# Moving the next image's statistics into the second convolution, and another order of what feeds both convolutions

## The chip, the core and the metric

One core of one Trainium2 chip runs the whole program: TensorE (PE, with its weight loads PEld), VectorE (DVE), ScalarE (ACT), GpSimd (POOL) and SyncE (SP), with 16 DMA engines. POOL issues transfers on the software queue q0, SP on the hardware queue q1. The metric is the device time of one launch in microseconds (us), as the median of several.

## The reference

The input x is 8 images of 96 channels x 96 x 96, all float32. Two blocks are applied in a row, each with a residual and a group norm (`_gn`, 32 groups of 3 channels) ahead of it:

```python
# block 0: four depthwise convolutions in four directions, mixed by a softmax, then a full 3x3 convolution
feats = stack([feat_h, feat_v, feat_d45, feat_d135])      # 7 taps each, per channel
context = mean(feats * feats, (3, 4))
attn = softmax(leaky_relu(context @ w_att1.T, 0.2) @ w_att2.T over the 4 directions)
x = x + conv3x3(sum(attn * feats), w_proj)
# block 1: linear attention whose output passes a 1x1, a depthwise 3x3 and further 1x1 matrices
x = x + _L1(_gn(x))
```

## The kernel before

**Two blocks, pipelined over images.** Call the images b = 0 to 7. A step of the loop does block 0 of image b and block 1 of image b-1 side by side. Each block ends in a 3x3 convolution on PE, written in `conv` (L1048). It runs over NG = 12 row groups of 8 rows; a row group j is two halves of 4 rows, and a half is 9 matmuls on `e_hi`, 9 on `e_lo` and 3 on `shifted`. The **second convolution** (weights `a1, a2, a3`, source line L1064 with `a`) closes block 1 of image b-1; the **first convolution** (weights `wp1, wp2, wp3`, L1064 with `wp`) closes block 0 of image b and comes right after it on PE.

**One step in time.** (1) PE runs the attention work of image b-1 while DVE adds taps of image b (L806: 4 directions, 6 taps each, in 12 units of 12 taps; a unit is two directions of one of NCH = 6 chunks of 16 rows). (2) PE runs the second convolution, DVE units 9 to 11, and between its taps DVE splits the exponentials into `e_hi` and `e_lo` (`e_split`, 24 tiles, the last 14 here). (3) `hidden` and `logits` (L1215, L1222) are small matmuls that PE does at row group 11 of the second convolution, between its halves; DVE waits for them in `attention` and turns them into the four mixing factors. (4) `products` (L928, L938) mix the four directions chunk by chunk: the feature maps come back from DRAM (`feats_d`, 20 loads of 576 KB by SP), the sum goes to the buffer `acc`, ACT rounds it to `e_hi` (`fg_high`, L669), DVE computes `e_lo` (`fg_low`, L944). (5) PE runs the first convolution on them. After each row group DVE adds the residual (`x1_sum`, L896) and takes statistics (L900). `SUMS_AFTER` says how many of these stand behind each chunk's products, the rest follow in `start`. (6) `start` of the next image: six loads of x into `feat` (L378), sums and sums of squares by ACT (`x_sums`, L531, two passes a load), group norm on DVE with one small matmul on PE (L1046) and one power on POOL (L416), then `norm_chunk` (L553) and `first_tap` (L573) on ACT, and the first 20 taps on DVE, with the rest of the `x1_sum` between them. (7) The group norm of the sum x1 (L765 on), and the next attention begins.

**Order.** Each engine runs its instructions in the order of its program; there is no scheduler. What links them is semaphores. For a row group j of either convolution PE waits (`ready`) for five transfers by POOL (`fill`, L426): two bulk copies of 32 partitions (L431, L432) and three ring transfers into `shifted` (L435), whose two slots come free when row group j-2 is done. From row group 2 on the second convolution also waits for `final_copy` (L651) of group j-2 on ACT, the first for `x1_sum` of group j-2 on DVE. POOL, behind each fill, also issues the stores of results and, in the first convolution, the loads of the residual (`res`). The buffer at `arena2` is shared in time by `s1`, `a32` and `acc`.

**What holds the change.** On ACT `final_copy` calls stand between `unit_work` of units 9, 10 and 11, which takes the squares of a unit (L585) and so waits for DVE's last taps of it.

## Time and profile before

| | us |
|---|---|
| median of 3 runs | 4011.15 (4006.11 to 4013.85) |
| the profiled execution | 4010.97 |
| its span | 4009.3 |
| PE busy | 3374.3 (84%) |
| DVE busy | 2954.0 (74%) |
| ACT busy | 1791.1 (45%) |
| POOL busy | 694.5 (17%) |

Times in the rows below are from the span's start. What the profiled execution adds to its span is 1.7 us, and it is within 0.2 us of the median. One full step (image 4, from 2009 us to 2480 us) is read closely; the others repeat it.

### The profile page before, as it was taken

To read this page: it belongs to the slowest core of one execution; us is meant where nothing else is said; L and a number is where in the kernel's file an instruction comes from. 1 tells how busy PE (TensorE), PEld (TensorE's weight loads), DVE (VectorE), ACT (ScalarE), POOL (GpSimd) and SP (SyncE) were. 2 spreads that over 40 slices of the span, in tenths; PEclk is the share of its full clock that TensorE was granted. 3 is DMA by queue.
4 is the path that set the end of the run, shared out by engine and by line. 5 is a ranking of instruction groups with operands and counts; after the bars stand their busy time and mean duration, and the time that the engine had idled before them with its cause. 6 is when DMAs were issued, how large, how long until landed. Compare 5 with 4: busy or idle time off the path is not lost.

```text
span 4009.3 us, 56727 instructions
## 1 busy us (share of the span) xinstructions
PE 3374.3 (84%) x20626; PEld 2713.3 (68%) x20626; DVE 2954.0 (74%) x2721; ACT 1791.1 (45%) x2921; POOL 694.5 (17%) x1336
## 2 busy tenths in 40 slices
PE   4648998699976999679986899869997799968998
PEld 2336687568765687666875677756876668757787
DVE  6976987579865998569984698758986599844211
ACT  5423682238623384135831467223861348410550
POOL 1013003220132102230022200322013200223003
PEclk9768999799998999889997999979998899989999
DMA  4367224943259324692338622494235923376004
GB/s 105 94 145 179 64 74 84 212 120 79 70 103 234 80 74 90 133 214 62 74 80 181 165 65 74 92 225 113 68 83 109 221 78 78 78 146 151 1 11 86
DMA packets 210824, 440.70 MB, mean 110 GB/s; under 512 B 125696, under 2 KB 125936, under 8 KB 210512
## 3 DMA queue, kind: packets, MB, share of 16 engines
q1 hardware_dynamic: 141392, 255.36, 26.3%
q0 software_dynamic: 69120, 181.32, 21.3%
q8 instruction: 179, 2.93, 0.3%
q14 instruction: 133, 1.09, 0.1%
HBM read 189.27 MB, written 150.99 MB: 85 GB/s over the span
## 4 chain that ended last, share of the span: by engine, by line
PE 31%; DVE 31%; issue 24%; DMA 10%; ACT 2%; POOL 1%; DVEq 0%; SPq 0%; ACTq 0%; POOLq 0%
DVE feat L806 22%; DMA feat<-feats_d 8%; PE banks L1083 6%; PE banks L1064 4%; PE banks L1069 4%; PE banks L1093 3%; PE banks L1151 3%; PE banks L1113 2%; PE banks L1099 2%; PE banks L1100 2%; DVE acc L938 2%; DVE feat L938 2%; DVE x L896 1%; PE banks L1073 1%; DMA shifted<-e_hi 1%
## 5 line engine op out<-in xcount | busy, mean ns | idle before, releaser
L806 DVE SCALAR_TENSOR_TENSOR feat<-xin,w,feat 96x1536 f32<-96x1536 f32 x540 | 947.0, 1807 | 1.8
L1064 PE MATMUL banks<-e_hi,wp 128*96 128x384 f32 x1728 | 397.5, 382 | 356.2 <-DMA shifted<-e_hi 240.5
L1064 PEld LDWEIGHTS banks<-e_hi,wp 128*96 128x96 f32 x1728 | 314.2, 186 | 408.0 <-issue 243.5
L585 ACT ACTIVATE squares<-feat 96x1536 bf16<-96x1536 f32 x192 | 285.1, 1485 | 589.2 <-DVE feat L806 587.0
L806 DVE SCALAR_TENSOR_TENSOR feat<-xin,wh,feat 96x1536 f32<-96x1536 f32 x288 | 520.3, 1807 | 30.1 <-ACT feat L573 28.4
L806 DVE SCALAR_TENSOR_TENSOR feat<-xin,wv,feat 96x1536 f32<-96x1536 f32 x288 | 520.3, 1807 | 0.0
L1064 PE MATMUL banks<-e_hi,a 128*96 128x384 f32 x1728 | 360.9, 356 | 106.7 <-ACT res L651 106.0
L1064 PEld LDWEIGHTS banks<-e_hi,a 128*96 128x96 f32 x1728 | 289.8, 170 | 149.5 <-ACT res L651 96.7
L1069 PE MATMUL banks<-e_lo,wp 128*96 128x384 f32 (+1 forms) x1728 | 369.7, 363 | 0.0
L1069 PE MATMUL banks<-e_lo,a 128*96 128x384 f32 (+1 forms) x1728 | 350.4, 349 | 0.0
L1069 PEld LDWEIGHTS banks<-e_lo,wp 128*96 128x96 f32 x1728 | 310.2, 180 | 32.6
L1093 PEld LDWEIGHTS banks<-mats,z 96*96 96x96 f32 x3072 | 287.3, 165 | 57.5 <-issue 46.7
L1069 PEld LDWEIGHTS banks<-e_lo,a 128*96 128x96 f32 x1728 | 292.5, 170 | 29.1
L1137 PE MATMUL banks<-wkv,x 97*96 97x96 f32 x3072 | 295.9, 249 | 0.9
L669 ACT ACTIVATE e_hi<-acc 96x1536 fp32r<-96x1536 f32 x48 | 71.4, 1488 | 497.6 <-DVE acc L938 497.6
L1093 PE MATMUL banks<-mats,z 96*96 96x96 f32 x3072 | 289.8, 248 | 2.5 <-ACT z L614 2.5
L435 POOL DMA_DIRECT2D shifted<-e_hi x576 | 285.7, 517 | 9.6 <-issue 9.4
L1137 PEld LDWEIGHTS banks<-wkv,x 97*96 97x96 f32 x3072 | 278.6, 165 | 10.4 <-issue 6.0
L421 POOL MEMSET e_hi<- 96x97 f32 x9 | 1.6, 176 | 1498.0 <-PE banks L1153 1498.0
L431 POOL DMA_DIRECT2D e_hi<-e_hi x192 | 100.1, 521 | 824.2 <-PE banks L1073 410.6
L651 ACT ACTIVATE res<-banks 96x768 f32<-96x768 f32 x96 | 74.8, 801 | 358.8 <-PE banks L1073 358.8
L815 DVE TENSOR_REDUCE mx<-banks 96x1 f32<-96x512 f32 x288 | 185.1, 681 | 42.1 <-PE banks L1083 41.9
(161 smaller groups left out, 5456.3 us busy)
## 6 DMA issues: line engine op xcount, KB each, us to landing
feats_d<-feat SPq DMA_DIRECT2D x160, 576.0 KB, 4.1
feat<-feats_d SPq DMA_DIRECT2D x160, 576.0 KB, 8.4
shifted<-e_hi POOLq DMA_DIRECT2D x576, 97.2 KB, 2.7
feat<-in_x SPq DMA_DIRECT2D x48, 576.0 KB, 9.5
res<-in_x POOLq DMA_DIRECT2D x96, 288.0 KB, 4.7
out<-x POOLq DMA_DIRECT2D x96, 288.0 KB, 2.9
out<-res POOLq DMA_DIRECT2D x96, 288.0 KB, 4.4
xin<-in_x SPq DMA_DIRECT2D x32, 792.0 KB, 8.7
```

The lines of the kernel that those rows point to most:

```text
L431: pool.dma_start(e_hi[C:C + SPARE, lo:hi], e_hi[0:SPARE, lo:hi]).then_inc(done, 16)
L435: pool.dma_start(shifted[g * SPARE:(g + 1) * SPARE, j % 2, :], e_hi[2 * SPARE:C, at:at + SHIFTED])\
L585: act.activation(squares[0 if first_image(b) or u <= LEAD else 1][:], feat[:, d], ACT.Square, accum_out=sq[:, d, ch:ch + 1]).then_inc(squa ...
L806: dve.scalar_tensor_tensor(out=dst, in0=src, scalar=taps_w[d](k), in1=dst, op0=ALU.mult, op1=ALU.add).then_inc(tap_done, 1)
L815: dve.tensor_reduce(mx[:, n % 2, n // 2:n // 2 + 1], stage_ps[0:C, n % SLOTS, :], AX.X, ALU.max)\
L938: ins = dve.scalar_tensor_tensor(out=flat if k == DIRS - 1 else part, in0=feat[:, d], scalar=l0v[:, 8 + d:9 + d], in1=part, op0=ALU.mult, ...
L1064: pe.matmul(dst, w1[:, t, :], rows(e_hi, a0, n, dx, 128), start=(t == CENTRE_FIRST[0]), stop=False)
L1069: pe.matmul(dst, w2[:, t, :], rows(e_lo, a0, n, dx, 128), start=False, stop=False)
L1083: pe.matmul(ps[0:C, :], w, x1[0:C, t * BANK:(t + 1) * BANK], start=True, stop=True)\
L1093: last = pe.matmul(ps[0:H, c * W:(c + 1) * W], z[:, 4 * g + c, :], w_dft, start=(c == 0), stop=(c == 3), skip_group_check=True)
L1137: last = pe.matmul(ps[0:W, r * C:(r + 1) * C], x1[:, h * W:(h + 1) * W], wkv[:, part * C:(part + 1) * C], start=(r == 0), stop=(r == TR - ...
L1151: pe.matmul(gram_ps[0:C, 2 * C:4 * C], t_sp[:, v, 0:C], t_sp[:, v, :], start=(v == 1), stop=(v == NV - 2))
```

## The change

- **ACT's order in the second convolution.** The final copies stand 3, 4, 3 ahead of the work of units 9, 10, 11 where 2, 2, 2 stood (`COPIES_AFTER`).
- **The next image's x.** Its six loads go no longer to `feat` at the end of the step but, one at a time, to `xc`, which lies where `acc` lies; ACT sums them after the final copies 1, 3, 4, 5, 7 and 8 (`CHUNKS_AT`). The passes' other output goes to PSUM, no longer to `squares`. SP issues the first after `a32` is free, each further one after the sums of the one before; the stores of unit 9 stand between the second and the third. The first write of `acc` waits for the last sums. Only image 0 keeps the old way.
- **The fills.** The three ring transfers of a row group come first, and the two bulk copies behind them are those of the next row group; each kind has its own semaphores.
- **DVE.** `SUMS_AFTER` is 0, 0, 1, 2, 1, 1 for 0, 0, 0, 1, 1, 1; the group norm of x stands after six `x1_sum`, where it stood after five, and PE's matmul for it goes to row group 7. The tiles of `e_split` stand behind taps 1, 2, 4, 5, 7, 8, 10, 11 of a unit, where they stood behind 2, 4, 6, 8, 10, 12.

```diff
-SUMS_AFTER = (0, 0, 0, 1, 1, 1)
-GN_AT = sum(SUMS_AFTER) + 2
+SUMS_AFTER = (0, 0, 1, 2, 1, 1)
+GN_AT = sum(SUMS_AFTER) + 1
+CHUNKS_AT = (1, 3, 4, 5, 7, 8)
+COPIES_AFTER = (3, 7, 10)
...
+        xc = nc.alloc_sbuf_tensor_at("xc", [C, CR * W], F32, offset=s0)
...
+            def load_xc(b, n, second):
+                x = image(a["x"], b + 1)
+                if n >= 1:
+                    sp.wait_ge(x_stat, 2 * ((b + 1) * NCH + n))
+                elif second:
+                    sp.wait_ge(l1_small, b * L1_SMALL)
+                else:
+                    sp.wait_ge(wp_ready, LO_PARTS)
+                sp.dma_start(xc[:], x[:, n * CR * W:(n + 1) * CR * W]).then_inc(xc_loaded, 16)
...
                 for u in range(UNITS - 2):
+                    if more and u == UNITS - 3:
+                        load_xc(b, 0, second)
+                        load_xc(b, 1, second)
...
+                for n in range(2, NCH if more else 0):
+                    load_xc(b, n, second)
...
             def fill_e(i, j):
...
-                fill(e_filled, j)
+                e_rows(i, j)
+                shift(e_shifted, j)
+                for n in range(0 if j == 0 else j + 1, min(NG, j + 2)):
+                    e_rows(i, n)
+                    copy(e_copied, n)
...
+            def x_sums(b, n, x, junk):
+
+                for k, func in enumerate((ACT.Identity, ACT.Square)):
+                    wait(act, x_stat, 2 * (b * NCH + n) + k)
+                    act.activation(junk, x, func, accum_out=xsums[:, k, n:n + 1]).then_inc(x_stat, 1)
+
+            def next_x_sums(b, n):
+                act.wait_ge(xc_loaded, (b * NCH + n + 1) * 16)
+                x_sums(b + 1, n, xc[:].rearrange("p (b n) -> p b n", n=BANK), stage_ps[0:C, 2:SLOTS])
...
             def start(b):
-                if not first_image(b):
-                    x_sums(b)
                 norm_chunk(b, 0)
...
                 for u in range(LEAD + 1, UNITS):
-                    copies(j, j + 2)
-                    j += 2
+                    for n in range(j, COPIES_AFTER[u - LEAD - 1]):
+                        copies(n, n + 1)
+                        if more and n + 1 in CHUNKS_AT:
+                            next_x_sums(b, CHUNKS_AT.index(n + 1))
+                    j = COPIES_AFTER[u - LEAD - 1]
                     if first:
                         unit_work(b, u)
...
                         if k == DIRS - 1:
+                            if ch == 0 and more:
+                                dve.wait_ge(x_stat, 2 * (b + 2) * NCH)
+                                apart(dve)
```

ACT in the second convolution of a full step, before, from the second final copy on (L651; L585 squares, L573 first taps of unit 11):

```order
L651 ACTIVATE res<-banks 96x768
L583 REGISTER_ALU
L585 ACTIVATE squares_64,sq<-feat 96x1536
L583 REGISTER_ALU
L267 REGISTER_ALU
L585 ACTIVATE squares_64,sq<-feat 96x1536
L573 ACTIVATE feat<-xin,w 96x1536
L565 REGISTER_ALU
L573 ACTIVATE feat<-xin,w 96x1536
L648 REGISTER_ALU
L651 ACTIVATE res<-banks 96x768
```

The same place of the changed kernel (L686 is the final copy, L561 the sums, L620 the squares):

```order
L686 ACTIVATE res<-banks 96x768
L683 REGISTER_ALU
L686 ACTIVATE res<-banks 96x768
L564 REGISTER_ALU
L270 ISA
L561 ACTIVATE banks,xsums<-xc 96x1536
L270 REGISTER_ALU
L561 ACTIVATE banks,xsums<-xc 96x1536
L618 REGISTER_ALU
L620 ACTIVATE squares_65,sq<-feat 96x1536
```

The third final copy and the sums of one load of x now stand ahead of unit 9's squares.

DVE between the products of chunks 3 and 4 of a full step, before (L938 products, L928 the next chunk's first, L944 `fg_low`, L896 and L900 `x1_sum`):

```order
L938 SCALAR_TENSOR_TENSOR acc<-feat,l0v 96x1536
L926 ISA
L928 TENSOR_SCALAR feat<-feat,l0v 96x1536
L944 TENSOR_TENSOR e_lo<-acc,e_hi 96x16x96
L893 ISA
L894 ISA
L896 TENSOR_TENSOR x<-banks,res 96x768
L900 BN_STATS x1stats<-x 96x6 x2
```

There, in the changed kernel (L977, L964, L983, L932 and L936 are the same operations):

```order
L977 SCALAR_TENSOR_TENSOR acc<-feat,l0v 96x1536
L964 TENSOR_SCALAR feat<-feat,l0v 96x1536
L982 REGISTER_ALU
L983 TENSOR_TENSOR e_lo<-acc,e_hi 96x16x96
L929 REGISTER_ALU
L932 TENSOR_TENSOR x<-banks,res 96x768
L936 BN_STATS x1stats<-x 96x6 x2
L929 REGISTER_ALU
L932 TENSOR_TENSOR x<-banks,res 96x768
L936 BN_STATS x1stats<-x 96x6 x2
```

Before, this is the first `x1_sum`; now it is the second and the third, and the first stands one chunk earlier.

POOL in the middle of the second convolution, before (one row group and its store):

```order
L431 DMA e_hi<-e_hi 32x776
L432 DMA e_lo<-e_hi 32x776
L435 DMA shifted<-e_hi 32x778 x3
L480 ISA
L480 DMA out<-res 96x768
```

The same in the changed kernel:

```order
L444 DMA shifted<-e_hi 32x778 x3
L456 REGISTER_ALU
L452 DMA e_hi<-e_hi 32x776
L453 DMA e_lo<-e_hi 32x776
L512 ISA
L512 DMA out<-res 96x768
```

The ring transfers have moved ahead of the bulk copies, which are the next row group's.

## Rows read from the trace of the kernel before

**Rows 1.** The page: the chain that ended last, share of the span by engine.

```profile
PE 31%; DVE 31%; issue 24%; DMA 10%; ACT 2%; POOL 1%; DVEq 0%; SPq 0%; ACTq 0%; POOLq 0%
```

**Rows 2.** Waits, whole span: waiter, its releaser, us in total, times, longest.

```profile
DVE hid L909 <- PE banks L1215: 179.5, 8, 26.2
...
PE banks L1064 <- ACT res L651: 106.0, 21, 8.3
```

**Rows 3.** PE, second convolution, image 4: start, us, instructions [idle before <-releaser].

```profile
2028.63 1.70 PE L1064 MATMUL banks<-e_hi,a 128*96 128x384 f32 x9
...
2062.60 2.44 PE L1064 MATMUL banks<-e_hi,a 128*96 128x384 f32 x9 [4.13 <-ACT res L651]
...
2107.00 3.19 PE L1064 MATMUL banks<-e_hi,a 128*96 128x384 f32 x9 [6.77 <-ACT res L651]
...
2131.47 0.52 PE L1215 MATMUL banks<-l0v,att 96*48 96x1 f32 x8
```

**Rows 4.** PE, the last second convolution (image 7), its first and last matmuls.

```profile
3905.98 1.70 PE L1064 MATMUL banks<-e_hi,a 128*96 128x384 f32 x9 [0.26 <-DVE a L742]
...
3994.56 0.69 PE L1073 MATMUL banks<-shifted,a 96*96 96x384 f32 x3
```

**Rows 5.** ACT in the second convolution, image 4.

```profile
2054.27 1.49 ACT L585 ACTIVATE squares<-feat 96x1536 bf16<-96x1536 f32 x1 [9.89 <-DVE feat L806]
...
2060.28 1.57 ACT L573 ACTIVATE feat<-xin,w 96x1536 f32<-96x1536 f32 x1 [0.46 <-DMA feats_d<-feat]
2061.76 1.48 ACT L651 ACTIVATE res<-banks 96x768 f32<-96x768 f32 x2
```

**Rows 6.** PE, first convolution: four rows of image 4, one of image 7.

```profile
2156.61 2.95 PE L1064 MATMUL banks<-e_hi,wp 128*96 128x384 f32 x9 [16.31 <-DMA shifted<-e_hi]
...
2179.83 0.71 PE L1073 MATMUL banks<-shifted,wp 96*96 96x384 f32 x3
2190.05 3.19 PE L1064 MATMUL banks<-e_hi,wp 128*96 128x384 f32 x9 [9.52 <-DVE x L896]
...
2217.18 3.19 PE L1064 MATMUL banks<-e_hi,wp 128*96 128x384 f32 x9 [5.16 <-DMA shifted<-e_hi]
...
3613.59 3.17 PE L1064 MATMUL banks<-e_hi,wp 128*96 128x384 f32 x9 [11.64 <-DVE x L896]
```

**Rows 7.** DVE from the products on, image 4.

```profile
2138.10 1.01 DVE L928 TENSOR_SCALAR feat<-feat,l0v 96x1536 f32<-96x1536 f32 x1
...
2189.05 0.95 DVE L896 TENSOR_TENSOR x<-banks,res 96x768 f32<-96x768 f32 x1
...
2211.18 1.76 DVE L944 TENSOR_TENSOR e_lo<-acc,e_hi 96x1536 fp32r<-96x1536 f32 x1 [1.56 <-ACT e_hi L669]
...
2235.47 0.16 DVE L758 TENSOR_REDUCE mv<-xsums 96x2 f32<-96x12 f32 x1 [7.04 <-ACT squares L531]
...
2239.11 0.16 DVE L782 SCALAR_TENSOR_TENSOR xpar<-gstat,xpar 96x1 f32<-96x1 f32 x1
...
2292.35 0.80 DVE L765 BATCH_NORM_AGGREGATE mv<-x1stats 96x2 f32<-96x144 f32 x1 [0.16 <-DVE x1stats L900]
```

**Rows 8.** Stretch, us, PE, PEld, DVE, ACT, POOL busy, PEclk, DMA share, GB/s.

```profile
2029.00:2140.00 111.00, 95.82 (x520) 85.69 (x518) 78.54 (x79) 21.22 (x27) 34.24 (x61) 0.94 0.45 86
```

**Rows 9.** DMA from 2029 to 2140 us: issues, KB each, median us to landing.

```profile
shifted<-e_hi POOLq DMA_DIRECT2D x30, 97.2 KB, 2.4
feats_d<-feat SPq DMA_DIRECT2D x2, 576.0 KB, 4.0
```

**Rows 10.** DMA from 2141 to 2211 us (products): total, queue's share, ring transfers.

```profile
DMA packets 3907, 16.72 MB, mean 239 GB/s; under 512 B 793, under 2 KB 793, under 8 KB 3904
...
q1 hardware_dynamic: 2330, 12.33, 73.0%
...
shifted<-e_hi POOLq DMA_DIRECT2D x15, 97.2 KB, 7.3
```

**Rows 11.** DMA from 2211 to 2240 us: one load of the next image's rows.

```profile
xin<-in_x SPq DMA_DIRECT2D x1, 792.0 KB, 19.8
```

91 lines of the change are left out of this document (47 added, 44 removed).

## The prediction

> **What bounds the kernel now.** I read the page's chain first: it is split evenly between PE and DVE [rows 1], so no engine's total is the limit, and each stretch of a step has to be read for the wait that ends last. The list of waits names two that hang together [rows 2]: in the second convolution PE waits 21 times (three times in each of images 1 to 7) for ACT's final copy, 106.0 us in all, and DVE waits 179.5 us for `hidden`, the small matmul that stands behind eleven row groups of that convolution. PE's rows give the size [rows 3]: the convolution starts at 2028.63 and reaches `hidden` at 2131.47, 102.8 us for eleven row groups. The same work without anything beside it takes 3995.25 - 3905.98 = 89.3 us for twelve, 7.45 us each [rows 4]. So 102.8 - 82.0 = 20.8 us per step are lost: about 15.2 us idle and the rest matmuls after each idle time at the lower clock (2.44 and 3.19 us for nine, against 1.70). ACT's rows say why [rows 5]: with the third row group finished, ACT stands at unit 9's squares, which DVE's taps release at 2054.27, then at a first tap that waits for a store until 2060.28, and copies only at 2061.76. The other two waits have the same cause at units 10 and 11.
>
> The first convolution is held by other things. Its start waits 16.31 us for its fills, its third row group 9.52 us for the first `x1_sum`, its fifth 5.16 us for a ring transfer [rows 6]. DVE's side [rows 7]: that `x1_sum` stands at 2189.05, one chunk late; the last `fg_low` at 2211.18; then DVE waits 7.04 us for ACT's sums of x, and from the factors of the group norm (2239.3) to the group norm of x1 (2292.35) it is DVE's own taps and sums that fill 53.1 us. The DMA engines are full in the products [rows 10]: 16.72 MB at 239 GB/s.
>
> **Change, second convolution (images 1 to 7).** Start PE at 2028.6, a row group every 7.45 us: groups 0 to 11 end at 2036.1, 2043.5, 2051.0, 2058.4, 2065.9, 2073.3, 2080.8, 2088.2, 2095.7, 2103.1, 2110.6, 2118. Group j+2 needs copy j. Now ACT: copies 0 to 2 and two loads' sums (two passes of 1.5 us each, like the squares [rows 5]) are done by 2054.9. Unit 9 ends on DVE 1.5 us later than before, since 8 splits of 0.74 us stand in it for 6, so its squares, the store and the first taps end near 2063.4; copy 3 is done at 2064.3, needed at 2065.9. That is the tightest place, 1.6 us. Copy 4 and the third load's sums fit before 2073.3. A load of 576 KB lands in about 4.0 us, as the stores do [rows 9], and is issued only after the sums before it, so a load and its sums take some 7.2 us, just inside a row group. Units 10 and 11 end near 2083 and 2104; copy 7 comes at 2089 (needed 2095.7), copy 9 at 2104 (2110.6). All three waits go. Unit 11's squares end at 2107.4, so `hidden` isn't late either: 2110.7. What is late next is DVE's taps with their squares, 3 us behind.
>
> What it may cost: the DMA engines. Their share is 0.45 of 111 us [rows 8], 50 us. Six loads add 3.5 MB; at 0.73 x 70 us for 12.33 MB [rows 10] that is 4.1 us of the engines per MB, 14.7 us. 65 us in 91 us, and near 0.85 in the row groups where a load is always under way. A ring transfer lands 2.4 us after its issue here [rows 9] and 7.3 us in the full stretch [rows 10]; issued 2.4 us after the group before last has ended, it is in time up to 5.0 us. The new order gives it 1 us that the two bulk copies took. Best case nothing, worst case 2.3 us in three groups: 0 to 7 us a step. I take 1.5 us, since the mean share stays under 1 and nearer to rows 9. Passes that write PSUM stand in no row; from the 1.49 us of the squares up to twice that there is room, since ACT has 21 us of work in 111 [rows 8] and gets 18 more; I take 1.5 us. Gain: 20.8 - 1.5 = 19.3 us a step, 14 to 20.8, times 7 = 135 us.
>
> The Trainium skill bears on that cost ("DMA: Bandwidth & Descriptors", section "Queues, rings and completion order"): each DMA engine takes turns between the queues that have work, a packet at a time. By that rule a ring transfer of POOL doesn't stand behind a whole load of SP but moves at about half speed beside it, near 5 us instead of 2.4, an estimate from this page and rows 9, and the sum would be the same within 1.5 us a step; were transfers served in order of issue, it would be 2.4 + 4.0 = 6.4 us, and some groups would wait 1.4 us.
>
> **Change, first convolution with a next image (images 0 to 6).** In the times of before, where the products start at 2138.1 [rows 7]. The first `x1_sum` moves behind chunk 2, so the third row group starts at 2180.5, when the second has ended [rows 6], not at 2190.05. The next waits at 2190.1 for the second `x1_sum` (DVE's place of 2189.05, [rows 7]); then 7.45 us each. The seventh group waits for the fifth `x1_sum`, behind the last `fg_low`. That ended at 2212.9; two more sums of 1.9 us now lie in the products, partly in their idle time: 2215.8. At the lower clock it ends at 2224.5. PE's small matmul for the norm of x stands right there, x's sums being long done; the factors follow near 2226.6, against 2239.3. From there DVE has 53.1 us less one sum (five in that stretch, not six): 51.1. So 2277.7 against 2292.35: 14.6 us. Loads of the next `xin` rows took 19.8 us [rows 11] behind the loads of x; those are gone from there, and ACT's norm finds its rows.
>
> Against it: the products run at the DMA engines' limit, and PE, now two row groups further on, has POOL move 2.1 MB more (per group five transfers of 97.2 KB, a residual load and a store of 288 KB each) before the last chunk has come. At 239 GB/s that is up to 8.9 us, at least none. I take 2.6, since only the last two of five chunks are met. Gain 12 us a step, 5.7 to 16, times 7 = 84 us. The two taps left between the last `x1_sum` and the group norm of x1 are in the 51.1 us. Two more terms are hidden: the split order (DVE's total is the same) and the sums' wait on each other (0.2 us a pass).
>
> **Image 7** has no next one. Its third row group waits 11.64 us for the first `x1_sum` [rows 6]; PE sets the end. The moves save that, less what the later sums take: 11 us, 5 to 14. The last second convolution and the attention stretches stay. Sum: 135 + 84 + 11 = 230 us from 4011.0, which is also the median: about 3780.
>
> **Rivals.**
> (a) The DMA engines take the first convolution's gain back: full extra traffic (8.9 us) and ring transfers landing in 7.3 us, so that groups wait again. Gain 4 us a step, 5 in image 7: 4011 - 135 - 28 - 5 = 3843. For it: rows 10; against it: 3.5 MB leave just this stretch. The skill's rule above speaks for this rival: POOL's earlier packets take turns with SP's loads.
> (b) The chain of loads and sums is slower than a row group and holds the copies: two of three waits return in part, 8 us gain a step there: 4011 - 56 - 84 - 11 = 3860.
> (c) The copies are no longer the last to come, but a ring transfer or bulk copy holds the same groups, and the second convolution gains nothing: 4011 - 95 = 3916. The moved copies don't do what they are for. Against it: the 20.8 us of rows 3 are used up by ACT's three waits and the lower clock behind them, so no transfer is late there now.
> (d) Slower. The single buffer `xc` makes six loads and sums one chain from 2031.4, and `hidden` comes a copy and a row group (9 us) after the sixth. If a load takes L, `hidden` is at 2031.4 + 6 (L + 3.1) + 9. It eats both gains (2131.5 + 12) from L = 14.1 us. At the 19.8 us of [rows 11] it is 2177.8, 46 us late: 7 x (46 - 12) = 238 us slower, less 11: 4238. Against it: the DMA share of 0.45 [rows 8].
>
> **Numbers.** Forecast 72%, (a) 12%, (b) 8%, (c) 5%, (d) 3%. The forecast's own range is 4011 - 7 x 20.8 - 7 x 16 - 14 = 3739 to 4011 - 7 x 14 - 7 x 5.7 - 5 = 3868, which takes in (a) and (b). I give 3739 to 3865, some 85%; (c) and (d) are left out. A measurement here tells 0.2%, 8 us, from no change: faster 96%, same 1%, slower 3%.
>
> **What would show it.** In the changed profile: no PE wait for the final copy (106.0 us now); DVE's wait for `hidden` about 4 us a step; the second convolution near 91 us; PE's wait for the first `x1_sum` gone, fewer waits for ring transfers after the products; from products' start to the group norm of x1 142 us, not 154. I am wrong if ACT waits long for `xc`, if ring transfers land later than 5 us in the second convolution, or if the products take over 80 us, not 73.

## The result and the profile after

The changed kernel takes 3845.14 us (median of 4 runs, 3841.72 to 3853.25) against 4010.16 us for the kernel before in 4 runs, a ratio of 0.9592 with a 95% interval of 0.9573 to 0.961. So 165 us are gained, not the 230 us of the forecast. The profiled execution took 3853.25 us, the slowest of the four; its span is 3851.7 us, 157.6 us less than before. The work below accounts for those 157.6 us. One run of an experiment (e2_old_x) took 5625.12 us at a granted clock of 0.555, in the slow state of the chip, and is left out of that experiment's numbers.

First the page of the changed kernel: the chain that ended last, by engine, which answers to [rows 1].

```profile
PE 42%; DVE 23%; issue 19%; DMA 12%; ACT 2%; POOL 1%; SPq 0%; DVEq 0%; POOLq 0%; ACTq 0%
```

Both shares were 31% before. PE now has the largest one, 42%, and DVE 23%. The list of waits (waiter, releaser, us in total, times, longest) has these lines where [rows 2] stood:

```profile
PE banks L1103 <- DMA e_lo<-e_hi: 162.6, 14, 19.9
...
DVE feat L964 <- DMA feat<-feats_d: 130.0, 40, 6.3
...
PE banks L1085 <- DVE mv L803: 92.5, 8, 13.1
...
PE banks L1103 <- DMA shifted<-e_hi: 66.0, 30, 5.0
...
ACT banks L561 <- DMA xc<-in_x: 56.7, 21, 5.0
...
DVE gstat L811 <- PE banks L1085: 54.8, 16, 10.7
DVE l0v L942 <- ACT squares L620: 51.6, 8, 10.7
PE banks L1103 <- DVE x L932: 50.4, 12, 7.4
...
DVE hid L945 <- PE banks L1255: 25.9, 8, 3.6
```

PE's wait for the final copy (106.0 us in [rows 2]) no longer stands in the list. DVE's wait for `hidden` was 179.5 us in 8 times; it is 25.9 us now, 3.6 us at most. PE's rows of image 4 answer to [rows 3]; L1103 is the first line of a row group's matmuls (L1064 before), L1255 is `hidden`.

```profile
1965.73 1.70 PE L1103 MATMUL banks<-e_hi,a 128*96 128x384 f32 x9
...
2005.08 2.00 PE L1103 MATMUL banks<-e_hi,a 128*96 128x384 f32 x9 [2.04 <-DMA shifted<-e_hi]
...
2051.51 0.52 PE L1255 MATMUL banks<-l0v,att 96*48 96x1 f32 x8
```

The convolution starts at 1965.73 and reaches `hidden` at 2051.51: 85.8 us for eleven row groups, against 102.8 us. One wait is left in it, for a ring transfer. (Images 1 to 6 all have this wait, of 1.92 to 2.19 us; images 1, 2 and 5 have a second one of 0.7 to 1.3 us two row groups later.) ACT's rows of the same stretch answer to [rows 5]. L561 is a pass over a chunk of the next image, L686 the final copy, L620 the squares.

```profile
1988.13 0.81 ACT L686 ACTIVATE res<-banks 96x768 f32<-96x768 f32 x1 [6.66 <-PE banks L1112]
1988.84 1.44 ACT L561 ACTIVATE banks<-xc 96x1536 f32<-96x1536 f32 x1
...
2004.22 1.45 ACT L561 ACTIVATE banks<-xc 96x1536 f32<-96x1536 f32 x1 [2.19 <-DMA xc<-in_x]
...
2044.22 0.81 ACT L686 ACTIVATE res<-banks 96x768 f32<-96x768 f32 x1 [6.73 <-PE banks L1112]
2044.93 1.47 ACT L620 ACTIVATE squares<-feat 96x1536 bf16<-96x1536 f32 x1
```

ACT now waits for PE (6.66 us, 6.73 us) and not the other way round. From the products on DVE's rows answer to [rows 7]. L964 is the first product, L983 `fg_low`, L794 the moments of the next image, L811 and L818 its group norm, L801 the group norm of x1.

```profile
2058.14 1.02 DVE L964 TENSOR_SCALAR feat<-feat,l0v 96x1536 f32<-96x1536 f32 x1
...
2141.59 1.75 DVE L983 TENSOR_TENSOR e_lo<-acc,e_hi 96x1536 fp32r<-96x1536 f32 x1 [1.56 <-ACT e_hi L704]
...
2147.42 0.14 DVE L794 TENSOR_REDUCE mv<-xsums 96x2 f32<-96x12 f32 x1
...
2158.01 0.15 DVE L811 COPY gstat<-banks 96x2 f32<-96x2 f32 x1 [10.25 <-PE banks L1085]
...
2165.34 1.82 DVE L842 SCALAR_TENSOR_TENSOR feat<-xin,wh,feat 96x1536 f32<-96x1536 f32 x1 [3.10 <-ACT feat L608]
...
2209.47 0.80 DVE L801 BATCH_NORM_AGGREGATE mv<-x1stats 96x2 f32<-96x144 f32 x1
```

DVE no longer waits for ACT's sums (7.04 us in [rows 7]), but waits 10.25 us at L811 for PE's small matmul. PE's rows show why. The matmul (L1085) stands behind row group 6, whose first matmul had waited for its ring transfer; and at the end of the stage it is PE that waits 13.08 us for DVE.

```profile
2148.60 2.14 PE L1103 MATMUL banks<-e_hi,wp 128*96 128x384 f32 x9 [3.14 <-DMA shifted<-e_hi]
...
2157.65 0.25 PE L1085 MATMUL banks<-mv,mats 96*96 96x2 f32 x2
...
2210.57 0.48 PE L1085 MATMUL banks<-mv,mats 96*96 96x2 f32 x2 [13.08 <-DVE mv L803]
```

So the wait that ends last in this stage belongs to DVE: 10.25 us at L811 and 3.10 us for the first tap, while PE has time to spare.

Last a table of stages, read from such rows as the distance between named instructions (mean of images 1 to 6; "gram" is the last matmul of the attention stretch, "x1 norm" the group norm of x1). In brackets stand the experiments below. All are profiled executions.

| Kernel | image 0 up to `hidden` | gram to `hidden` | products, first to last `fg_low` | products to norm factors | products to x1 norm | image 7, products to x1 norm |
|---|---|---|---|---|---|---|
| before | 236.2 | 122.1 | 73.6 | 102.9 | 155.1 | 141.0 |
| after | 243.9 | 105.0 | 84.1 | 99.9 | 149.9 | 132.0 |
| (e1_copies_only) | 236.2 | 101.8 | 73.6 | 104.2 | 156.3 | 139.4 |
| (e2_old_x) | 235.7 | 101.3 | 83.6 | 109.0 | 160.4 | 133.5 |
| (e3_gn_row6) | 245.4 | 105.0 | 83.9 | 92.8 | 148.1 | 134.7 |
| (e4_xin_early) | 245.2 | 105.2 | 83.9 | 97.6 | 147.5 | 132.3 |
| (e6_old_sums) | 245.8 | 105.0 | 75.5 | 99.4 | 151.4 | 138.5 |
| (e7_old_fg_fills) | 246.3 | 105.4 | 79.4 | 98.3 | 148.2 | 129.0 |
| (e8_image0) | 237.0 | 104.5 | 84.6 | 98.9 | 148.9 | 134.4 |
| (e9_gn_inside) | 245.9 | 105.6 | 83.9 | 74.5 | 136.8 | 135.2 |
| (e13_gn_image0) | 235.8 | 105.2 | 83.2 | 73.8 | 136.2 | 135.5 |
| (e10_all) | 236.1 | 105.8 | 77.9 | 69.6 | 131.4 | 132.1 |
| (e11_half_res) | 244.9 | 104.7 | 80.4 | 97.4 | 147.3 | 131.7 |
| (e12_small_xc) | 240.0 | 101.3 | 83.3 | 98.6 | 148.5 | 131.1 |

The stages also tell how much one profiled execution differs from another. e8_image0 and e12_small_xc leave the first convolution of images 1 to 6 as it is, and its stage is 148.9 and 148.5 us there, against 149.9. A difference of 1 to 1.5 us in that column alone is not told from this spread.

The sum of the difference between before and after: second convolution 6 x 17.1 and 21.3 us in image 7, 124 us. First convolution with a next image: 7.6 us in image 0 and 6 x 5.2, 39 us; image 7 9.0 us. Less 7.7 us that image 0 loses in its first stretch, and 6 x 1.1 us of the attention stretches (190.3 before, 191.4 after). That is 157.7 us of the span's 157.6.

### The profile page after: what moved, and what is told of

The parts are those of the page before. It is cut to its first block, busy times and chain, and to the rows that moved or that the text cites. A ratio compares the mean times of both kernels' runs of the same rounds, so it can differ in the third digit from the quotient of the medians.

```text
span 3851.7 us, 57140 instructions
## 1 busy us (share of the span) xinstructions
PE 3318.3 (86%) x20626; PEld 2669.2 (69%) x20626; DVE 2952.3 (77%) x2721; ACT 1798.0 (47%) x2921; POOL 696.6 (18%) x1336
## 3 DMA queue, kind: packets, MB, share of 16 engines
q8 instruction: 179, 2.93, 0.3%
## 4 chain that ended last, share of the span: by engine, by line
PE 42%; DVE 23%; issue 19%; DMA 12%; ACT 2%; POOL 1%; SPq 0%; DVEq 0%; POOLq 0%; ACTq 0%
DVE feat L842 15%; DMA feat<-feats_d 9%; PE banks L1103 8%; PE banks L1108 8%; PE banks L1122 7%; PE banks L1132 3%; PE banks L1190 3%; PE banks L1112 3%; DVE feat L977 2%; DMA shifted<-e_hi 2%; PE banks L1152 2%; PE banks L1138 2%; PE banks L1139 2%; DVE x L932 1%; PE banks L1080 1%
## 5 line engine op out<-in xcount | busy, mean ns | idle before, releaser
L1103 PE MATMUL banks<-e_hi,wp 128*96 128x384 f32 x1728 | 380.2, 370 | 271.6 <-DMA e_lo<-e_hi 162.6
L1103 PEld LDWEIGHTS banks<-e_hi,wp 128*96 128x96 f32 x1728 | 302.7, 179 | 318.7 <-issue 237.1
L444 POOL DMA_DIRECT2D shifted<-e_hi x576 | 294.1, 521 | 891.6 <-PE banks L1112 479.1
L620 ACT ACTIVATE squares<-feat 96x1536 bf16<-96x1536 f32 x192 | 285.0, 1484 | 270.2 <-DVE feat L842 267.8
L1108 PE MATMUL banks<-e_lo,wp 128*96 128x384 f32 (+1 forms) x1728 | 360.7, 356 | 0.0
L1103 PE MATMUL banks<-e_hi,a 128*96 128x384 f32 x1728 | 341.1, 342 | 16.3 <-DMA shifted<-e_hi 13.1
L1108 PE MATMUL banks<-e_lo,a 128*96 128x384 f32 (+1 forms) x1728 | 337.6, 339 | 0.0
L1108 PEld LDWEIGHTS banks<-e_lo,wp 128*96 128x96 f32 x1728 | 302.2, 176 | 31.5
L1103 PEld LDWEIGHTS banks<-e_hi,a 128*96 128x96 f32 x1728 | 277.9, 163 | 52.8 <-issue 19.2
L1108 PEld LDWEIGHTS banks<-e_lo,a 128*96 128x96 f32 x1728 | 279.8, 163 | 26.1
L1176 PEld LDWEIGHTS banks<-wkv,x 97*96 97x96 f32 x3072 | 278.6, 165 | 10.5 <-issue 6.1
L686 ACT ACTIVATE res<-banks 96x768 f32<-96x768 f32 x96 | 77.4, 806 | 379.2 <-PE banks L1112 378.8
L977 DVE SCALAR_TENSOR_TENSOR feat<-feat,l0v 96x1536 f32<-96x1536 f32 x96 | 173.8, 1810 | 48.3 <-DMA feat<-feats_d 47.0
```

The lines of the kernel that those rows point to most:

```text
L444: pool.dma_start(shifted[g * SPARE:(g + 1) * SPARE, j % 2, :], e_hi[2 * SPARE:C, at:at + SHIFTED])\
L620: act.activation(squares[0 if first_image(b) or u <= LEAD else 1][:], feat[:, d], ACT.Square, accum_out=sq[:, d, ch:ch + 1]).then_inc(squa ...
L977: ins = dve.scalar_tensor_tensor(out=flat if k == DIRS - 1 else part, in0=feat[:, d], scalar=l0v[:, 8 + d:9 + d], in1=part, op0=ALU.mult, ...
L1103: pe.matmul(dst, w1[:, t, :], rows(e_hi, a0, n, dx, 128), start=(t == CENTRE_FIRST[0]), stop=False)
L1108: pe.matmul(dst, w2[:, t, :], rows(e_lo, a0, n, dx, 128), start=False, stop=False)
L1176: last = pe.matmul(ps[0:W, r * C:(r + 1) * C], x1[:, h * W:(h + 1) * W], wkv[:, part * C:(part + 1) * C], start=(r == 0), stop=(r == TR - ...
```

## The experiments

Each run is timed against the kernel before on the same chip. The ratio of the changed kernel to compare with is 0.9592. The changed kernel was not run again beside the experiments, which were measured on three chips, so the stages of the table decide where the ratios are close.

**The order of ACT's copies by itself** (e1_copies_only). The kernel before with one edit:

```diff
-                    copies(j, j + 2)
-                    j += 2
+                    copies(j, (3, 7, 10)[u - LEAD - 1])
+                    j = (3, 7, 10)[u - LEAD - 1]
```

> The kernel before with one edit: the final copies stand 3, 4 and 3 ahead of the work of units 9, 10 and 11. Theory: ACT's order alone held the second convolution. From the gram matmul to `hidden` a step took 122.1 us before and takes 105.0 us in the changed kernel with a next image, 101.3 us without one; here it should be 101.3 us in all seven, since no x is loaded there: 7 x 20.8 = 146 us, 4010 to about 3865, and the first convolution as before (155 us from the products' start to the group norm of x1). Rival: part of the gain came from the ring transfers, which here still stand behind two bulk copies: then row groups wait for them and it is 108 us or more, 3910 or above.

Measured: 3876.55 us (3872.46 to 3877.96) against 4015.27 us, ratio 0.9653, interval 0.9636 to 0.967. These two lines give 139 us; 146 were expected. The stretch up to `hidden` is 101.8 us, 20.3 us less than before, and within 0.5 us of what image 7 shows with nothing beside it (101.3 us). So the three waits for ACT were, within 0.5 us, the whole loss of the second convolution, as rows 3 and 5 had it, and nothing else takes their place. The new order of the fills is not needed for it; whether it is needed beside the loads of x was not tested. The first convolution, which this edit leaves alone, is 1.2 us longer a step, within the spread.

**The change with x loaded and summed the old way** (e2_old_x). The changed kernel, where the six loads of the next image's x go into the feature slots behind the products' loads again, with their sums behind ACT's last `e_hi`:

```diff
-                for n in range(NCH if first_image(b) else 0):
+                for n in range(NCH):
...
-                        if more and n + 1 in CHUNKS_AT:
-                            next_x_sums(b, CHUNKS_AT.index(n + 1))
...
             def start(b):
+                if not first_image(b):
+                    all_x_sums(b)
                 norm_chunk(b, 0)
```

> The changed kernel with x handled as before (six loads into `feat` at the end of the step, sums in `start`), everything else changed. Theory A: in the changed kernel the factors of the group norm wait for PE's row group 7 and not for x, so taking x back costs little there (factors at 101 to 103 us after the products' start, as in both kernels), while the second convolution loses its loads (105.0 to 101.3 us, 22 us in all) and image 0 gets its 7.7 us back: 3845 to about 3820 to 3835, faster than the changed kernel. Rival B: the x loads are what makes the transfers of the first convolution late; putting them back costs up to 12 us a step: 3900 or above.

Measured: 3888.67 us (3886.34 to 3900.14, three runs), ratio 0.9683, interval 0.9663 to 0.9704. Theory A was wrong: the factors come at 109.0 us and not at 101 to 103. The move of x is a gain, and this kernel is slower than the one with the copies alone (0.9653), by 12 us. DVE's row in image 4, the moments of the next image (L795 here), where [rows 7] has 7.04 us:

```profile
2185.21 0.16 DVE L795 TENSOR_REDUCE mv<-xsums 96x2 f32<-96x12 f32 x1 [16.53 <-ACT squares L567]
```

The first convolution takes 160.4 us here against 149.9 us with x moved: moving x is worth 10.5 us there, less 3.7 us in the second convolution (105.0 against 101.3), and less image 0's 8 us. It also shows that the rest of the first convolution's edits (sums, fills, place of the group norm) don't help a step with a next image by themselves: 160.4 against 156.3 us with the copies alone. They do help image 7, 133.5 against 139.4 us. And the products last 83.6 us with the old x as well; x's move isn't what made them longer.

**The group norm one row group earlier** (e3_gn_row6).

```diff
-{(GN_AT + 1, 0): lambda: start(b + 1)}
+{(GN_AT, 0): lambda: start(b + 1)}
```

> The changed kernel with PE's small matmul for the norm of x at row group 6, where it stood before, and not 7. DVE waited 10.25 us for it in image 4, from 2147.6. Theory: it is that wait which sets the factors; at row group 6 (2148.6) they come 9 us earlier, and the first taps then wait for the load of `xin`, which lands near 2156: 5 us a step, 7 steps, 3845 to about 3810. Rival: DVE and PE are bound otherwise before the group norm of x1 (row groups that wait for transfers), and it stays at 3845.

Measured: 3841.36 us, ratio 0.9565, interval 0.9548 to 0.9582. The factors come 7.1 us earlier (92.8 against 99.9), but 5.3 of them are given back behind them (55.3 us from the factors to the x1 norm, 50.0 before). DVE's rows in image 4, at the same lines as in the changed kernel (L932 is `x1_sum`):

```profile
2141.03 0.16 DVE L811 COPY gstat<-banks 96x2 f32<-96x2 f32 x1 [1.87 <-PE banks L1085]
...
2150.13 0.95 DVE L932 TENSOR_TENSOR x<-banks,res 96x768 f32<-96x768 f32 x1 [7.42 <-PE banks L1112]
```

The wait for PE at L811 is down to 1.87 us, and the next `x1_sum`, which stands in front of the first tap, waits 7.42 us for the row group that used to come first. What is won in all, 1.8 us a step, is hardly more than the spread, and far from the 5 us expected. The wait was moved, not removed: DVE has to have other work (taps) between the two.

**The next `xin` loads ahead of the products' loads** (e4_xin_early).

```diff
+                if more:
+                    load_xin(b + 1, 0)
+                    load_xin(b + 1, 1)
                 for ch in range(1, NCH):
```

(and `start` loads them for image 0 alone)

> The changed kernel with the two loads of the next image's `xin` ahead of the 20 product loads on SP, not behind them. They took 20 and 26 us to land behind them, about 10 us of the DMA engines' time. Theory: the DMA engines are what is late after the products; row groups 5 to 7 lose their waits for ring transfers (3.6 us in image 4), and PE reaches the matmul of the norm that much sooner: 25 us, 3845 to about 3820. Rival: the transfers compete with other work of POOL and not with SP's: no change, 3845.

Measured: 3836.7 us, ratio 0.9555, interval 0.9535 to 0.9574. The stage is 2.4 us shorter (147.5 against 149.9), the factors come 2.3 us earlier, and the products are not longer for it (83.9). In image 4 PE no longer waits for ring transfers at the sixth and seventh row groups (0.51 and 3.14 us in the changed kernel), so these loads, which took 20.4 and 25.9 us to land behind the products' loads, were part of what held that transfer. Some 15 us in all by the ratios, under the 25 us expected.

**The sums of x1 in their old places** (e6_old_sums).

```diff
-SUMS_AFTER = (0, 0, 1, 2, 1, 1)
-GN_AT = sum(SUMS_AFTER) + 1
+SUMS_AFTER = (0, 0, 0, 1, 1, 1)
+GN_AT = sum(SUMS_AFTER) + 2
```

> The changed kernel with the sums of x1 in the old places (none behind the third chunk of the products, one behind the fourth instead of two) and the group norm behind row group 4 plus two, as before. Question: why do the products last 83.5 us with the change and 73.5 us without it? Theory (the sums: two more of them stand inside the products, each 0.95 us plus 1.02 us and the wait for PE's row group): the products last 74 to 77 us here, the stretch from the first product to the x1 moments 148 to 151 us against 149 now, for the two sums come later and nothing is won; ratio 0.957 to 0.962. Rival (the new order of the bulk copies on GpSimd's queue lengthens them): the products still last 82 to 84 us and the stretch 158 us, ratio about 0.97.

Measured: 3869.94 us, ratio 0.9637, interval 0.9617 to 0.9657. The products last 75.5 us, so having the two sums in them is what makes them 8.6 us longer. The stage up to the x1 norm is only 1.5 us longer in this run, which is within the spread; what else the sums win lies in image 7, 138.5 against 132.0 us, where PE sets the end. The ratio is 18 us worse than the changed kernel's, of which the stages explain 6 x 1.5 + 6.5 = 15.5 us.

**The first convolution's fills in the old order** (e7_old_fg_fills).

```diff
                 fg_rows(b, j)
+                copy(fg_copied, j)
                 shift(fg_shifted, j)
-                if j == 0:
-                    copy(fg_copied, 0)
-                if j >= 1:
-                    for n in range(1 if j == 1 else j + 1, min(NG, j + 2)):
-                        fg_rows(b, n)
-                        copy(fg_copied, n)
```

> The changed kernel with the first convolution's fills in the old order (the two bulk copies of a row group ahead of its own ring transfers, none of them one group ahead); the second convolution's fills stay new. Theory of the sums: the products still last 82 to 84 us, the stretch to the x1 moments 149 us, within 2 us a step; ratio 0.956 to 0.961. Rival (bulk copies one group ahead compete with the products' loads, and are what cost 4 us a step in the run with the old x): the stretch falls to 145 us, some 28 us in all, ratio 0.952. The third case, that the new order helps PE there (its waits for the ring are 66.0 us in all now): the stretch grows by 2 to 5 us a step, ratio 0.962 to 0.967.

Measured: 3838.98 us, ratio 0.955, interval 0.9527 to 0.9574. The bulk copies made one group ahead cost the products 4.7 us (84.1 against 79.4), but only 1.7 us reach the end of the stage (149.9 against 148.2), for DVE waits for PE's small matmul anyway. In image 7, where nothing follows, 3.0 us do. The shorter products are clear, against the theory as I wrote it for this run (products unchanged). What they are worth in the time is not clear from this run, for 1.7 us a step is hardly more than the spread.

**Image 0's sums of the next x spread over its units 2 to 7** (e8_image0).

```diff
+                    if not second and 2 <= u < 2 + NCH:
+                        load_xc(b, u - 2, second)
...
                         unit_work(b, u)
+                        if not second and 2 <= u < 2 + NCH:
+                            next_x_sums(b, u - 2)
```

(and none of them at `CHUNKS_AT` in image 0)

> The changed kernel, where image 0's step sums the next image's six chunks one behind each of units 2 to 7, and asks for them ahead of those units' stores, instead of all six in front of the squares of the last units. Theory (ScalarE's sums and their waits of 4.3 to 5.0 us for loads in front of the squares of units 9 to 11 are what image 0 lost, 243.9 us against 236.2 us up to hidden): image 0's stretch goes back to 236 to 238 us, the rest stays; 5 to 8 us less in all, ratio 0.9575 against 0.9592. Rival (image 0's units are held by the loads of x itself beside the stores): 242 to 246 us as now, no gain.

Measured: 3834.93 us, ratio 0.9546, interval 0.9522 to 0.957. Image 0's stretch is 237.0 us, against 243.9. In the changed kernel ACT and DVE stand like this at its end, the squares being those of the last unit:

```profile
222.02 1.45 ACT L561 ACTIVATE banks<-xc 96x1536 f32<-96x1536 f32 x1 [4.24 <-DMA xc<-in_x]
...
229.55 1.45 ACT L561 ACTIVATE banks<-xc 96x1536 f32<-96x1536 f32 x1 [4.34 <-DMA xc<-in_x]
...
241.89 1.48 ACT L620 ACTIVATE squares<-feat 96x1536 bf16<-96x1536 f32 x1
...
243.50 0.17 DVE L942 TENSOR_REDUCE l0v<-sq 96x4 f32<-96x24 f32 x1 [10.70 <-ACT squares L620]
```

Image 0 has no final copies between the sums, so ACT ran through loads and sums in one chain in front of the squares, and DVE waited 10.70 us. With the sums spread out that wait is 3.31 us, and this stretch gives 6.9 us, as expected. The ratio is lower than the 0.9575 expected, by some 12 us. The stages put 6 us of the difference into the first convolutions of images 1 to 6 (1.0 us each) and 3.3 us into that of image 0, and no run shows a cause for either.

**The next group norm inside the products** (e9_gn_inside). From DVE's rows of the changed kernel (10.25 us and 3.10 us idle, PE with 13.08 us to spare) and from the runs with the earlier group norm and the earlier loads (each of which moved one end of it and ran into the other) comes this edit. The x sums are ready before the products begin, so the moments can stand behind the second chunk and the factors behind the fifth:

```diff
-GN_AT = sum(SUMS_AFTER) + 1
+GN_AT = 4
+MOMENTS_AFTER, FACTORS_AFTER = 1, 4
...
                         fg_high(b, ch)
+                        if more and ch == FACTORS_AFTER:
+                            norm_chunk(b + 1, 0)
+                            norm_chunk(b + 1, 1)
...
-                taps(b, 0, hooks=[(2, between), (6, between), (10, between)])
-                taps(b, 1, 0, EARLY_TAPS, hooks=[(2, between), (6, between)])
+                taps(b, 0, hooks=[(n, between) for n in (5, 8, 12)])
+                taps(b, 1, 0, EARLY_TAPS, hooks=[(n, between) for n in (3, 6)])
...
+                        if more and ch == MOMENTS_AFTER:
+                            gn = small_chain(dve, gnx_small, GN_SMALL, b + 1)
+                            moments_x(b + 1, gn)
                         for _ in range(SUMS_AFTER[ch]):
                             sums()
+                        if more and ch == FACTORS_AFTER:
+                            factors(b + 1, gn, gnx_ps, gnx_pow, 0, xpar)
...
-{(GN_AT + 1, 0): lambda: start(b + 1)}
+{(GN_AT, 0): lambda: start(b + 1)}
```

(`factors` is the second half of `group_norm`; the early `xin` loads are in it too)

> The changed kernel with the next image's group norm inside the products: its moments behind the second chunk, PE's 2 small matmuls in front of row group 4, the factors behind the fifth chunk, ScalarE normalises the next image's first two pieces behind its fifth copy of the products, the two first xin loads are issued ahead of the products' loads, and the last six sums of x1 stand behind 0, 5, 8, 12, 15, 18 and 20 of the next image's taps. Theory (DVE sets the end of this stage: it waits 10.3 us for PE's group norm sums and 3.1 us for the first tap, while PE is idle for 13.1 us ahead of the x1 moments): the stretch from the first product to the x1 moments falls from 149 to 137 to 141 us, then PE's row groups (7.5 us each) set its end; 56 to 84 us less in seven steps, ratio 0.937 to 0.945. Rival (PE's row groups or the DMA set the end already): no more than the 15 us that the early xin loads gave, ratio 0.955. Slower, if the norm on ScalarE holds back its sixth copy of the products: the stretch over 150 us.

Measured: 3764.94 us (3757.85 to 3769.76), ratio 0.9367, interval 0.9346 to 0.9388. The stage takes 136.8 us, 13.1 less than with the change as it was (the early loads by themselves gave 2.4). DVE's rows in image 4, with L829 in the factors, L995 `fg_low`, L854 a tap and L810 the x1 norm in this kernel:

```profile
2080.45 0.15 DVE L829 COPY xpar<-gpar 96x1 f32<-96x1 f32 x1 [0.75 <-POOL gpar L435]
...
2090.26 1.76 DVE L995 TENSOR_TENSOR e_lo<-acc,e_hi 96x1536 fp32r<-96x1536 f32 x1 [1.56 <-ACT e_hi L709]
...
2096.47 1.81 DVE L854 SCALAR_TENSOR_TENSOR feat<-xin,wh,feat 96x1536 f32<-96x1536 f32 x1
...
2142.75 0.80 DVE L810 BATCH_NORM_AGGREGATE mv<-x1stats 96x2 f32<-96x144 f32 x1 [0.16 <-DVE x1stats L948]
```

The first tap stands 6.2 us behind the last `fg_low`, without a wait, where it was 23.8 us (2165.34 - 2141.59). From the last `fg_low` to the x1 norm DVE has nothing but its own work. Image 7, which has no next group norm, takes 135.2 us, 3.2 more than in the changed kernel; no run shows a cause.

**All that helped, and the same without the old fills** (e10_all, e13_gn_image0). The group norm inside, image 0's sums spread out, and the first convolution's fills in the old order; the second kernel keeps the new fills. The diffs are those above.

> The group norm inside the products, image 0's sums behind its units 2 to 7, and the first convolution's fills in the old order, all in one. By the single runs: the group norm inside the products gives 2.3 points of ratio against the changed kernel, image 0's sums some 7 us (0.2 points). The fills shortened the products by 4 us a step, where that was hidden behind PE's group norm sums; here VectorE goes on with the next image's taps as soon as the products end, so if they set the end it shows now: the stretch from the first product to the x1 moments 132 to 134 us instead of 136.5, ratio 0.925 to 0.931. Rival: PE's row groups of 7.5 us take over as the bound, the last sum of x1 waits for PE, the stretch stays at 135 to 137 us, ratio 0.933 to 0.936.

> The run before without the old order of the first convolution's fills: the group norm inside the products and image 0's sums behind its units 2 to 7. It tells what the fills are worth there. Theory (they are worth 3 to 4 us a step now): ratio 0.934 to 0.936, the stretch to the x1 moments 136.5 us, 20 to 28 us more than with the old fills. Rival (PE is the bound in both): within 5 us of the run with the old fills.

Measured: with all three 3724.12 us (3719.39 to 3729.67), ratio 0.9279, interval 0.9256 to 0.9301; with the new fills 3751.81 us, ratio 0.9343, interval 0.932 to 0.9366. Both are as expected. The fills are worth 28 us here, 4.8 us a step (131.4 against 136.2), where the same edit gave 1.7 us before. The end of the products was covered by DVE's wait at L811, and with that wait gone it shows. So the new order of the first convolution's fills is a loss. The first of the two is the fastest kernel of the study, 121 us under the changed kernel by the medians. PE's last wait of the stage in it, its small matmul for the x1 norm (L1099 here):

```profile
2114.02 0.48 PE L1099 MATMUL banks<-mv,mats 96*96 96x2 f32 x2 [2.93 <-DVE mv L811]
```

PE has 2.93 us to spare, of 13.08: the two engines are nearly even there.

**Half of the residual loads** (e11_half_res).

```diff
-                            pool.dma_start(res[:, j % RES], x[:, j * GR * W:(j + 1) * GR * W])\
+                            n = GR * W if first_image(b) else GR * W // 2
+                            pool.dma_start(res[:, j % RES, 0:n], x[:, j * GR * W:j * GR * W + n])\
```

> The changed kernel, but the residual loads of x for the sums of x1 bring only the first half of each row group from image 1 on (144 KB instead of 288 KB each; the second half keeps what the buffer held, so that part of the output is not the reference's). Some 1.0 MB of the 17.0 MB that lie in the products are gone, all waits and instructions stay. Theory (the DMA engines, busy all through the products, set their length): products 79 to 80.5 us instead of 83.5, the stretch to the x1 moments 3 to 4.5 us shorter, ratio 0.951 to 0.954. Rival (the chain on VectorE of load, product, slot free, next load sets it): products stay within 1 us, ratio 0.957 to 0.960.

Measured: 3836.41 us, ratio 0.9563, interval 0.9535 to 0.959. The products last 80.4 us, as expected, 3.7 us less for some 1.0 MB. A stretch bound by the DMA engines alone would give 4.4 us (1.0 of the 19.0 MB that image 4's products move in the changed kernel, times 84.1 us), and most of it came. In the eight other kernels with the same sums and fills in the products they last 83.2 to 84.6 us, so 80.4 is clear of the spread. The stage is 2.6 us shorter, less than the 3 to 4.5 us expected, and the ratio lies between the two theories' ranges. So the bytes moved set most of the products' length, and the rival (no more than 1 us) is refuted; the end of the stage hears less of it, for DVE waits for PE's small matmul there. These are windows of the changed kernel (columns as in [rows 8]): most of the products first, then their end and up to the factors, then the taps:

```profile
2058.10:2133.00 74.90, 43.07 (x202) 37.32 (x201) 50.78 (x39) 8.26 (x6) 23.05 (x43) 0.79 1.01 226
...
2133.00:2160.00 27.00, 23.34 (x123) 20.57 (x122) 10.39 (x17) 1.67 (x2) 7.59 (x15) 0.94 0.88 177
2160.00:2210.00 50.00, 37.48 (x205) 32.70 (x203) 46.68 (x40) 15.98 (x12) 14.06 (x28) 0.91 0.48 125
```

The DMA share is 1.01 for 75 us and 0.88 for the next 27.

**A third of each load of the next x** (e12_small_xc).

```diff
-                sp.dma_start(xc[:], x[:, n * CR * W:(n + 1) * CR * W]).then_inc(xc_loaded, 16)
+                sp.dma_start(xc[:, 0:BANK], x[:, n * CR * W:n * CR * W + BANK]).then_inc(xc_loaded, 16)
...
-                x_sums(b + 1, n, xc[:].rearrange("p (b n) -> p b n", n=BANK), stage_ps[0:C, 2:SLOTS])
+                x_sums(b + 1, n, xc[:, None, 0:BANK].broadcast_to([C, 3, BANK]), stage_ps[0:C, 2:SLOTS])
```

> The changed kernel, but the loads of the next image's x beside the second convolution bring a third of a chunk (192 KB instead of 576 KB), which ScalarE reads three times, so that its work stays the same (the next image's sums, and so its norm, are not the reference's). The second convolution's stretch is 105 us a step with these loads and 101.3 us where nothing of x is loaded or summed there. Theory (the loads' bytes hold PE's ring transfers: the wait of 2.04 us for the shifted rows at the convolution's start): the stretch falls to 102 to 103 us, some 15 us less in all, ratio 0.954 to 0.957. Rival (ScalarE's two passes a chunk beside PE, in PSUM, hold it): it stays at 104.5 to 105 us, ratio 0.957 to 0.960.

Measured: 3814.46 us, ratio 0.95, interval 0.9477 to 0.9522. The stretch up to `hidden` is 101.3 us in all of images 1 to 6, the length without any load or sum. ACT's passes are all still there, so they cost PE nothing; the 3.7 us are those of the loads' bytes. The windows of the changed kernel in image 4, around PE's one wait:

```profile
1990.00:2002.34 12.34, 12.34 (x71) 11.24 (x70) 12.34 (x15) 9.00 (x11) 4.71 (x9) 1.00 0.99 223
2002.34:2009.76 7.42, 5.38 (x23) 4.48 (x21) 7.42 (x8) 3.85 (x5) 4.13 (x7) 0.78 0.92 181
```

The first is the stretch ahead of the wait, with the DMA engines at 0.99. The second is one half row group: 7.42 us against 3.73 us for the others. Of the 3.69 us that it loses 2.04 are the wait, the rest the lower clock behind it (0.78 granted in this window). With the small loads a stretch that holds nearly the whole convolution (1943.81 to 2034.64) looks like this:

```profile
1939.60:2032.90 93.30, 93.27 (x523) 82.37 (x522) 80.02 (x83) 41.68 (x55) 33.55 (x61) 1.00 0.60 116
```

PE busy 93.27 of 93.30 us, clock 1.00, DMA share 0.60 (0.68 in the changed kernel's convolution, 1965.73 to 2060.33). The run's median is 31 us under the changed kernel's, more than these 6 x 3.7 us, and more than the 15 us expected: 3.9 us lie in image 0, where the loads stand in front of the squares, and 1.4 us a step in the first convolution, for which no run shows a cause.

## Why the prediction was right, and where its sizes were off

The time came 65 us above the forecast, inside the range. By the terms of the sum:

**Second convolution.** Forecast 19.3 us a step, 135 in all; measured 17.1 in six steps and 21.3 in image 7, 124 us. The mechanism is shown: the order of the copies alone gives 139 us. The forecast left out that image 7 has no next x to load; there the whole 20.8 us came back. In the others the cost of the loads, taken as 1.5 us, is 3.7 us, inside the bounds of 0 to 7. The mean share that I took (65 us of 91, 0.71; measured 0.68) was right, but it doesn't tell how late the worst transfer is. These are the DMA issues of the changed kernel from 1995 to 2005 us, KB each, median us to landing:

```profile
shifted<-e_hi POOLq DMA_DIRECT2D x6, 97.2 KB, 5.2
feats_d<-feat SPq DMA_DIRECT2D x1, 576.0 KB, 4.3
xc<-in_x SPq DMA_DIRECT2D x1, 576.0 KB, 8.2
```

Two stores of features (issued at 1992.88 and 1995.35, landed at 1997.35 and 1999.66) and a load of x (1995.96 to 2004.11) meet the ring transfers there. The median of six hides what PE waited for: the three transfers issued from 1996.25 on, on which its late row group depends, take 6.57, 7.07 and 7.45 us, and the three behind them 3.6 to 3.8 us. In images 1 to 6 the first three take 6.5 to 7.6 us. Over the whole convolution the median is 2.1 us, less than the 2.4 us of before [rows 9]. By the prediction's own sum a transfer is late from 5.0 us on, and these were. From 1996.25 to 1999.90, and then from 1999.90 to 2004.87 (the last landing), the view of the DMA queues has these lines (packets, MB, share of the engines' time):

```profile
q1 hardware_dynamic: 186, 0.96, 96.2%
...
q0 software_dynamic: 263, 0.57, 80.9%
q1 hardware_dynamic: 61, 0.28, 24.6%
```

In the first window there is no line for q0: for 3.65 us after POOL's first issue the engines moved SP's packets alone. With idle engines a ring transfer's first packet starts 1.1 us after its issue (issued at 1988.78, first packet at 1989.86). The rule of the Trainium skill that was cited ("DMA: Bandwidth & Descriptors", section "Queues, rings and completion order": an engine takes turns between its queues) led to an estimate near 5 us for a ring transfer beside a load, and the other case, transfers served in order, to 6.4 us. The trace does not agree with the first: 6.5 to 7.6 us is past both, and in the first window no turn went to q0. Both estimates reckoned with one transfer of 576 KB, where three overlap here. Whether q0's packets were ready earlier, and so whether the engines passed them over, no run shows. So the consequence drawn from the rule, "the same within 1.5 us", was too small, and a wait of 2.04 us costs 1.65 us of lower clock as well.

**ACT's passes into PSUM.** Taken as 1.5 us, 1.44 to 1.45 us measured, and by the run with small loads they cost PE nothing.

**First convolution with a next image.** Forecast 12 us a step, 84 in all; measured 39 us (5.2 a step in images 1 to 6, below my bound of 5.7; 7.6 in image 0). This is the step that failed. Two of its parts came out: from the factors to the x1 norm 51.1 us forecast, 50.0 measured, and ACT's norm finds its rows. The first is in part luck: I read the 53.1 us of before as DVE's own taps and sums, but 4.29 us of them were its wait for ACT's first tap; it is 3.10 us in image 4 now, which was in no term.

What failed is the time of the factors. Forecast were 88.5 us after the first product (2226.6 - 2138.1) and 2.6 us of DMA cost, 91.1 us; measured were 99.9 us, 8.8 us late. Of these 5.5 us lie in the products. Their last `fg_low` was to end 77.7 + 2.6 = 80.3 us after the start, and ends at 84.1 + 1.7 = 85.8 us. I had 2.9 us for the two more sums and 2.6 us for the traffic, 5.5 us together, and the products got 10.5 us longer. The term that was mis-sized is the traffic, taken as 2.6 us of at most 8.9. These are the DMA queues' lines from the first product to the last `fg_low` of image 4, before (2138.10 to 2211.18) and after (2058.14 to 2141.59):

```profile
q1 hardware_dynamic: 2333, 12.33, 70.0%
q0 software_dynamic: 1586, 4.39, 29.2%
...
q1 hardware_dynamic: 4032, 12.48, 66.2%
q0 software_dynamic: 2288, 6.48, 36.2%
```

SP's queue moves what it moved; POOL's moves 2.1 MB more, as much as the prediction counted, at the same rate in all (229 GB/s before, 228 after), with the engines full in both. That is 9.1 us (2.09 MB at 229 GB/s). The reason for taking less, "only the last two of five chunks are met", didn't hold. The runs bear it out: with the sums in their old places POOL's queue moves 3.71 MB in image 4's products, and they last 75.5 us in the mean; with half of the residual loads 5.60 MB and 80.4 us. With the old order of the fills it moves nearly as much as in the changed kernel (6.28 MB), but at 236 GB/s, and the products last 79.4 us; why the rate is higher was not separated. How much of the length comes instead from the sums holding back DVE's release of feature slots was not separated either. The halved residual loads, which leave every wait in place, speak for the bytes.

The other 3.3 us are PE's small matmul: forecast 10.8 us from the end of `fg_low` to the factors, measured 14.1 us. I had placed the row group in front of it as if its ring transfer were there; it waited 3.14 us for it in image 4, and DVE 10.25 us behind it. With the next `xin` loads issued early that wait is gone and the factors come 2.3 us sooner; the prediction has no cost for these loads.

**Image 7.** Forecast 11 us, measured 9.0.

**Image 0.** Forecast as a step like the others; it also lost 7.7 us in its first stretch, which stands in no term. The change puts the sums of the next x in front of image 0's last squares, and there no final copies and PE work cover them. I had looked at ACT's order for images 1 to 6 alone. The run with the sums spread out gives 6.9 us of it back.

**The attention stretches** were to stay, and are 1.1 us longer a step.

**The rivals.** (a) "DMA takes the first convolution's gain back" forecast 3843 us, and the time is 3845. Its mechanism is the one that held in the first convolution: the full extra traffic of 2.1 MB lies in the products, ring transfers land after 5 to 12 us there in image 4, and row groups still wait for them. It was given 12%, and its 4 us a step is nearer to the 5.2 measured than the forecast's 12. That its total fits within 2 us is in part luck: it had 135 us for the second convolution (124 measured), and no loss in image 0 or the attention stretches (14 us); the first convolutions gave 15 us more than its 33. (b), a chain of loads holding the copies, did not happen: ACT waits 2.19 and up to 5.0 us for `xc`, and PE waits for no copy. (c) is refuted by the run with the copies alone. (d), slower, would have needed 14.1 us a load; they land after 5.1 us (median of 42).

**The signs that I named**, in their order: no wait of PE for the final copy, right. DVE's wait for `hidden` about 4 us, 3.6 at most. The second convolution near 91 us: 94.6 us in image 4 (1965.73 to 2060.33), the two small matmuls in it. PE's wait for the first `x1_sum` gone: half right, it is 2.44 us at the third row group and 5.98 us at the fourth. Fewer waits for ring transfers after the products: right in image 4, one (3.14 us) where there were five. But PE's waits for fills in all are hardly less, 162.6 + 66.0 us where they were 240.5, since the first row group still waits 17.12 us, now for a bulk copy. From the products' start to the x1 norm 142 us: 149.9. Of the three signs of being wrong, ACT's waits for `xc` stayed short (5.0 us at most) and held no copy that PE waited for. Ring transfers did land later than 5 us in the second convolution, in one place a step. The products over 80 us is what happened too, and it is where most of the missing gain went.

## What to carry to other kernels

When work is moved into a stretch that the DMA engines fill, price it by the transfers that it sets off, at the rate of that stretch, and not by its own length: 3.8 us of sums made this stretch 5.8 to 8.6 us longer. A wait behind an engine's queue is only gone when the engine has other work in its place: the earlier group norm alone gave 1.8 us a step, hardly more than the spread, and with taps put between it and the next sum, and its small operations inside the products, 13.1 us. And an edit that is worth little while a later wait covers it (the old fills, 1.7 us a step) has to be tried again when that wait is gone (4.8 us).
